# Layer 3 of the last pair but one in layer 0's banks and buffers, and an order of its own for the last periods

## The reference

```
x = L0(x, adj)   8 heads, masked softmax(q k^T), four hops z = 0.9 P z + 0.1 v, then layer norm of x + z
x = L1(x, adj)   1 head: softmax(x Wq Wk^T x^T / 16) x Wv Wo + bo, then layer norm of x + that
x = L2(x, adj)   8 heads, softmax(q k^T / sqrt(32)) v, times Wo, then layer norm
x = L3(adj, x)   labels 1..4 of adj: weight_d = (adj == d) / count, agg = concat_d(weight_d^T x)
                 out = relu(agg Wd + bd)
                 r = sigmoid(out Wri + x Wrh), z = sigmoid(out Wzi + x Wzh)
                 n = tanh(out Wni + r * (x Wnh)), y = (1 - z) n + z x, then layer norm
```

## Time and profile before

| | us |
|---|---|
| median of three runs (1607.26 to 1608.85) | 1607.68 |
| span of the profiled execution, first to last instruction | 1605.4 |
| PE busy | 1547.1 (96%) |
| DVE busy | 1282.8 (80%) |
| ACT busy | 1237.9 (77%) |
| POOL busy | 697.0 (43%) |

### The profile page before, as it was taken

How to read it: one execution, slowest core, us unless ns; L and a number is a source line. 1 busy time by engine, 2 the same in 40 slices (tenths; PEclk the granted TensorE clock), 3 DMA queues, 4 the chain that set the end, 5 groups by cost and what they waited for, 6 DMA issues and landing times.

```text
span 1605.4 us, 44598 instructions
## 1 busy us (share of the span) xinstructions
PE 1547.1 (96%) x17360; PEld 1405.8 (88%) x17360; DVE 1282.8 (80%) x3164; ACT 1237.9 (77%) x4074; POOL 697.0 (43%) x710
## 2 busy tenths in 40 slices
PE   7888999999999999999999999999999999999986
PEld 6777999899899989998998999899899999998875
DVE  3676888888888888888888888888888888888764
ACT  4677887787888788888878788887878888787652
POOL 1344444434454444445444444544444444444411
PEclk7999999999999999999999999999999999999999
DMA  5100000111110011011001101100110110000000
GB/s 201 34 25 28 28 28 15 34 35 29 34 35 28 15 35 34 28 35 35 27 15 35 35 28 35 34 28 15 35 35 28 35 35 27 15 28 25 18 8 13
DMA packets 71425, 51.64 MB, mean 32 GB/s; under 512 B 4400, under 2 KB 69936, under 8 KB 70576
## 3 DMA queue, kind: packets, MB, share of 16 engines
q1 hardware_dynamic: 71216, 48.79, 10.0%
HBM read 40.39 MB, written 8.39 MB: 30 GB/s over the span
## 4 chain that ended last, share of the span: by engine, by line
PE 67%; ACT 28%; DVE 2%; issue 1%; DMA 1%; POOL 0%; SPq 0%; POOLq 0%; DVEq 0%; ACTq 0%
ACT E L706 9%; PE bank_A L400 7%; ACT E L770 7%; PE bank_B L400 7%; PE bank_B L629 6%; PE bank_A L444 6%; PE bank_C L400 5%; PE bank_B L444 4%; PE bank_A L629 3%; PE bank_A L418 3%; PE bank_B L412 3%; ACT PT L712 2%; PE bank_A L430 2%; PE bank_X L550 2%; PE bank_A L528 2%; PE bank_B L438 2%
## 5 line engine op out<-in xcount | busy, mean ns | idle before, releaser
L850 POOL TENSOR_TENSOR E<-E,rsum 128x512 f32<-128x512 f32 x256 | 270.7, 1058 | 472.5 <-DVE rsum L1041 317.6
L858 POOL TENSOR_TENSOR rstd<-var,minus_half 128x2 f32<-128x2 f32 x128 | 93.7, 741 | 407.9 <-DVE var L995 407.9
L712 ACT ACTIVATE PT<-bank_C 128x512 f32<-128x512 f32 x128 | 85.8, 670 | 59.9 <-PE bank_C L438 59.9
L1002 DVE TENSOR_SCALAR y<-y,mv,rstd 128x256 f32<-128x256 f32 x192 | 93.0, 527 | 25.8 <-POOL rstd L858 25.8
L943 DVE COPY_PREDICATED_SCALAR bank_A<-absent,fill 128x512 f32 x128 | 92.3, 742 | 15.2 <-PE bank_B L430 14.4
L400 PE MATMUL bank_A<-xT_hi,w_hi 128*128 128x256 f32 x384 | 99.7, 284 | 0.0
L400 PE MATMUL bank_A<-xT_hi,w_lo 128*128 128x256 f32 x384 | 97.1, 277 | 0.0
L943 DVE COPY_PREDICATED_SCALAR bank_B<-absent,fill 128x512 f32 x128 | 94.7, 740 | 0.0
L770 ACT ACTIVATE E<-bank_A,nmax 128x128 f32<-128x128 f32 x256 | 92.4, 402 | 2.5 <-DVE nmax L1037 2.5
L706 ACT ACTIVATE E<-bank_B,nmax 128x128 f32<-128x128 f32 x256 | 94.2, 435 | 0.0
L706 ACT ACTIVATE E<-bank_A,nmax 128x128 f32<-128x128 f32 x256 | 90.8, 382 | 4.1 <-DVE nmax L946 4.1
(11 more groups left out here) (225 smaller groups left out, 6299.3 us busy)
## 6 DMA issues: line engine op xcount, KB each, us to landing
xt_in<-in_xt SPq DMA_DIRECT2D x64, 128.0 KB, 2.3
absent<-in_adj SPq DMA_DIRECT2D x64, 128.0 KB, 2.7
x_in<-in_x SPq DMA_DIRECT2D x32, 256.0 KB, 3.0
out<-y SPq DMA_DIRECT2D x32, 256.0 KB, 2.2
adj<-in_adj SPq DMA_DIRECT2D x32, 128.0 KB, 3.3
adjT<-in_adjt SPq DMA_DIRECT2D x32, 128.0 KB, 3.1
stage<-in_weights SPq DMA_DIRECT2D x3, 1024.0 KB, 11.3
row<-in_rows SPq DMA_DIRECT2D x1, 1024.0 KB, 7.9
```

The lines of the kernel that those rows point to most:

```text
L712: nc.scalar.activation(PT0[:, part].rearrange("p g c n -> p (g c n)"), C0[:, :], ACT.Copy, scale=1.0 - ALPHA).then_inc(pt0_ready.sem, 1)
L850: nc.gpsimd.tensor_tensor(e, e, rs[:, part].unsqueeze(2).to_broadcast([P, SB, P]), ALU.mult).then_inc(e_sig.sem, 1)
L858: nc.gpsimd.tensor_tensor(rstd[part][:], var[part][:], minus_half[:], ALU.pow)\
L1002: a = nc.vector.tensor_scalar(y[part][:, g, :], src[g], mv[part][:, g, 0:1], rstd[part][:, g:g + 1], ALU.subtract, ALU.mult)
```

## The change

Three things change. First, layer 3's buffers and banks become a named tuple `Layer3`, of which there are two: `main`, the old ones, and `spare`, which lies in layer 0's banks A0 and B0 and in layer 0's buffers (`PT0`, `E0`, `qT0`, `kT0`, `zT0`, `nmax0`, `esum0`, `x_in`). `layer3(it)` gives `spare` for pair 30 (`SPARE = ROUNDS - 2`) and `main` for all others. Where `n3` and `cnt` waited for the pair before, `wait_free3` lets pair 30 wait for `y_sum[0]` of pair 31 (the end of layer 0 of the last pair), and pair 31 for pair 29. Second, the periods from 32 on no longer come from `ORDER`: each engine has a list `TAIL`, in which `lab@1` means step `lab` of the pair one before the last. Third, the eight entries of `IDLE` in the second half of the run go, with their 92 transposes.

```diff
 IDLE = {("p0", 0, 0): 10, ("n1", 0, 0): 12, ("g1", 0, 0): 10, ("p0", 2, 1): 17, ("p1", 0, 0): 9,
-        ("g1", 0, 1): 17, ("p0", 2, 2): 17, ("p0", 3, 2): 8, ("g1", 0, 2): 17, ("p0", 2, 3): 17, ("p0", 3, 3): 8,
-        ("n2", 0, ROUNDS - 1): 8, ("mixt", 0, ROUNDS - 3): 10, ("out", 0, ROUNDS - 2): 7,
-        ("mixt", 0, ROUNDS - 2): 12, ("n3", 0, ROUNDS - 1): 18, ("lab", 0, ROUNDS - 1): 17,
-        ("out", 0, ROUNDS - 1): 7, ("mixt", 0, ROUNDS - 1): 13}
+        ("g1", 0, 1): 17, ("p0", 2, 2): 17, ("p0", 3, 2): 8, ("g1", 0, 2): 17, ("p0", 2, 3): 17, ("p0", 3, 3): 8,}
+TAIL_FROM = 32
+TAIL = {
+    "tensor": [
...
+        "lab.2@2 cnt@1 lab.3@2 agg.2@2 s02.1@-2 agg.3@2 lab@1 out@2 lab.1@1 agg@1 nh@2 p2 lab.2@1 rh@2 agg.1@1 ri@2",
+        "agg.2@1 p2.1 lab.3@1 ni@2 p2.2 p2.3 z@2 agg.3@1 hop2 hop2.1 out@1 cnt wo2 mixt@2 wo2.1 rh@1 nh@1 ri@1 ni@1",
+        "n3 z@1 lab lab.1 agg agg.1 lab.2 lab.3 agg.2 mixt@1 agg.3 out nh rh ri ni z mixt",
...
+SPARE = ROUNDS - 2
+Layer3 = namedtuple("Layer3", "A B BA xT xT_hi xT_lo xw_hi xw_lo agg oT oT_hi oT_lo rT zT nT degree rcnt y")
 def periods(engine):
 
     steps = table(engine)
-    for n in range(ROUNDS + LAST_LAG):
+    for n in range(TAIL_FROM):
         for step, part, lag in steps:
             if 0 <= n - lag < ROUNDS + EXTRA.get(step, 0):
                 yield step, part, n - lag
+    for token in " ".join(TAIL[engine]).split():
+        name, _, back = token.partition("@")
+        step, _, part = name.partition(".")
+        yield step, int(part or 0), ROUNDS - 1 - int(back or 0)
...
+        main = Layer3(A3, B3, (B3, A3), xT3, xT_hi[3], xT_lo[3], xw_hi, xw_lo, agg, oT, oT_hi, oT_lo, rT, zT, nT,
+                      degree, rcnt, y[3])
+        spare = Layer3(A0, B0, (B0, A0), sx, sx_hi, sx_lo, s_hi, s_lo, s_agg, so, so_hi, so_lo, qT0, kT0, zT0,
+                       s_degree, s_rcnt, x_in)
+        def layer3(it):
+            return spare if it == SPARE else main
...
+        def wait_free3(eng, signal, it, k):
+            if it == SPARE:
+                wait(eng, y_sum[0], ROUNDS - 1, G)
+            elif it > SPARE:
+                wait(eng, signal, it - 2, k)
+            else:
+                wait_before(eng, signal, it, k)
...
                     wait(pe, nrm_ready[2], it, 1)
-                    wait_before(pe, nrm_ready[3], it, 1)
-                    transpose_y(A3, y[2]).then_inc(n_t[3].sem, 1)
+                    wait_free3(pe, nrm_ready[3], it, 1)
+                    transpose_y(layer3(it).A, y[2]).then_inc(n_t[3].sem, 1)
```

More of the change, by code:

```diff
@@ L1 @@
+from collections import namedtuple
 from contextlib import ExitStack
@@ L92 @@
 }
+TAIL_FROM = 32
+TAIL = {
+    "tensor": [
[6 rows of a table added]
+    ],
+    "scalar": [
[8 rows of a table added]
+    ],
+    "gpsimd": [
[4 rows of a table added]
+    ],
+    "vector": [
[14 rows of a table added]
+    ],
+    "sync": [
+        "ld_adj.2@2 ld_x@1 ld_adj.1@1 ld_adj.3@3 ld_adj ld_adj.1 ld_adj.3@2 ld_adj.2@1 store@5 ld_x ld_adj.2 store@4",
+        "ld_adj.3@1 ld_adj.3 store@3 store@2 store@1 store",
+    ],
+}
 def table(engine):
@@ L627, in _ @@
                     for kc in range(NC):
-                        for j, (a, w) in enumerate(((xT_hi, w_hi), (xT_lo, w_hi), (xT_hi, w_lo))):
-                            mm = nc.tensor.matmul(BA3[part % 2][:, :], a[3][:, kc, g * P:(g + 1) * P],
+                        for j, (a, w) in enumerate(((at.xT_hi, w_hi), (at.xT_lo, w_hi), (at.xT_hi, w_lo))):
+                            mm = nc.tensor.matmul(at.BA[part % 2][:, :], a[:, kc, g * P:(g + 1) * P],
                                                   w[:, n:n + 2, kc, :], start=kc == 0 and j == 0,
@@ L637, in _ @@
                     for d in range(2):
-                        for xs in (xw_hi, xw_lo):
-                            mm = nc.tensor.matmul(BA3[part % 2][:, d * D:(d + 1) * D], wT[it % 2][:, g, 2 * pair + d],
-                                                  xs[:, part % 2, d], start=xs is xw_hi, stop=xs is xw_lo)
+                        for xs in (at.xw_hi, at.xw_lo):
+                            mm = nc.tensor.matmul(at.BA[part % 2][:, d * D:(d + 1) * D], wT[it % 2][:, g, 2 * pair + d],
+                                                  xs[:, part % 2, d], start=xs is at.xw_hi, stop=xs is at.xw_lo)
                     mm.then_inc(agg_t.sem, 1)
@@ L721, in _ @@
                     L = int(step[-1])
-                    bank = (None, X1, A2, A3)[L]
+                    bank = (None, X1, A2, layer3(it).A)[L]
                     wait(act, n_t[L], it, 1)
                     if step[:2] == "hi":
-                        to, ready = xT_hi[L], xhi_ready[L]
+                        to, ready = x_hi_of(L, it), xhi_ready[L]
                     else:
@@ L728, in _ @@
                             wait_before(act, o2, it, G)
-                        to, ready = xT[L], xt32[L]
+                        to, ready = x_of(L, it), xt32[L]
                     for c in range(NC):
@@ L794, in _ @@
                     wait(act, agg_t, it, 2 * part + 1)
-                    nc.scalar.activation(agg[:, part], BA3[0][:, 0:D], ACT.Copy,
-                                         scale=rcnt[:, part, 0:1]).then_inc(first_sum.sem, 1)
+                    nc.scalar.activation(layer3(it).agg[:, part], layer3(it).BA[0][:, 0:D], ACT.Copy,
+                                         scale=layer3(it).rcnt[:, part, 0:1]).then_inc(first_sum.sem, 1)
                 if step == "lab":
@@ L802, in _ @@
                         wait(act, agg_t, it, part - 1)
-                    nc.scalar.activation(xw_hi[:, part % 2].rearrange("p d f -> p (d f)"), BA3[part % 2][:, :],
+                    nc.scalar.activation(layer3(it).xw_hi[:, part % 2].rearrange("p d f -> p (d f)"),
+                                         layer3(it).BA[part % 2][:, :],
                                          ACT.Copy).then_inc(xw_hi_ready.sem, 1)
@@ L861, in _ @@
                     i = (0, 1, None, 2)[part]
-                    to = (xn[0], xn[1], None, y[3])[part]
+                    to = (xn[0], xn[1], None, layer3(it).y)[part]
                     if step == "sc":
@@ L978, in _ @@
                 if step in ("bn", "nrm"):
-                    src = [A3[:, g * D:(g + 1) * D] if part == 3 else y[part][:, g, :] for g in range(G)]
+                    src = [layer3(it).A[:, g * D:(g + 1) * D] if part == 3 else y[part][:, g, :] for g in range(G)]
                 if step == "bn":
@@ L998, in _ @@
                     wait(dve, rstd_ready[part], it, 1)
-                    if part == 3:
+                    if part == 3 and it != SPARE:
                         wait_before(dve, stored, it, 16)
+                    to = layer3(it).y if part == 3 else y[part]
                     for g in range(G):
-                        a = nc.vector.tensor_scalar(y[part][:, g, :], src[g], mv[part][:, g, 0:1],
+                        a = nc.vector.tensor_scalar(to[:, g, :], src[g], mv[part][:, g, 0:1],
                                                     rstd[part][:, g:g + 1], ALU.subtract, ALU.mult)
@@ L1063, in _ @@
                     wait(dve, counted, it, 1)
-                    count = B3[:, 0:2 * G * LABELS].rearrange("p (g d two) -> p g d two", g=G, d=LABELS)
-                    nc.vector.tensor_scalar(degree[:], count[:, :, :, 0], DEG_EPS, None, ALU.add)\
+                    count = layer3(it).B[:, 0:2 * G * LABELS].rearrange("p (g d two) -> p g d two", g=G, d=LABELS)
+                    nc.vector.tensor_scalar(layer3(it).degree[:], count[:, :, :, 0], DEG_EPS, None, ALU.add)\
                         .then_inc(guarded.sem, 1)
```

83 lines of the change are left out of this document (51 added, 32 removed), and 29 rows, old and new, of the table TAIL.

## The result

The changed kernel takes 1596.24 us (median of four runs, 1592.98 to 1598.14), the kernel before 1608.26 (1607.26 to 1611.74): a ratio of 0.9919 with a 95% interval of 0.9901 to 0.9936, 12.0 us faster by the medians and 0.8% by the ratio. The forecast was 1592.0 in a range of 1585.5 to 1600.5. The profiled execution has a span of 1596.3 us and a time of 1598.14, 1.8 above it.

The account below looks back on a forecast made before the run. PE bounds the body, latency of layer 3 passes run one behind the other the end. `n3` of pair 31 at 1554.5, plus 34.8 and 0.4, ends the span at 1589.7; time 1592.0 us, range 1585.5 to 1600.5.

Parts of the forecast that it names:

- The last pass: Layer 3 of pair 31, from its `n3` to the end of the span: 34.8 us as before, plus 0.4.
- The start of the last pass: `n3` of pair 31, forecast at 1554.5 us: 1504.9 plus 44.1 of PE work, 4.3 of waits and 1.2 for handovers.
- the stretch that I took as unchanged: 1466.5 to 1504.9 us, up to `n3` of pair 29: same steps reordered, priced at 0, between −2.2 and +2 us.
- the recorded sum: PE work from `n3` of pair 29 to `n3` of pair 31: 17.2 + 14.0 + 11.0 + 1.9 = 44.1 us.
- The sum of the waits: PE's waits between `n3` of pair 29 and `n3` of pair 31, forecast at 4.3 us in all.
- the walk: Going through the four engines' lists with earlier durations to find PE's waits; it gave 4.3 us.
- The 1.2 us for handovers: Added before `n3` of pair 31 for handovers between engines taken as free at nine or ten places.
- The other branch: Layer 2's norm for pair 31, also needed before its `n3`: ready near 1553.1 us, level with PE at 1553.3.
- The clock: PE's granted clock without fillers: no cost but 0.3 us at the last `mixt`; upper end 7 us.
- half hidden: Rival, chance 0.12: layer 3's two passes block each other in DVE and ACT queues; `n3` of pair 31 at 1563.0, time 1600.5.
- the rivals: Besides half hidden: PE never waiting, 1584 (0.04); one clock fall, 1599 (0.05); clock staying low (0.04); no effect, 1607 (0.01).

## Why the prediction was right, and where its sum was off

**The mechanism.** It held: `n3` of pair 31, plus one pass, is the time, and the second pass of layer 3 beside the first moved that `n3` by 13.1 us. The banks alone gave a ratio of 0.9986, the fillers' removal alone a loss, and the order can't run without the banks.

**The last pass.** Forecast 35.2 us, measured 35.33. The last `mixt` at half the clock was named with 0.3 us and then left out of the sum; it cost 0.35. `bn.3` of pair 30 ahead of `acc.4` was put at 0.35: `out` waits 1.30 us for the last `acc`. The stretch from `n3` to the last `mixt` is 26.03 us against 25.91, so nearly all of that was hidden. `z` of pair 30 in the gap cost nothing, as forecast, and the experiment that takes it out of the gap lost 2.65.

**The start of the last pass.** From the mark the forecast was 1554.5 − 1413.7 = 140.8 us, measured 143.75: 3.0 us too soon. Half of it is the stretch that I took as unchanged. `n3` of pair 29 comes 92.52 us after the mark instead of 91.15, because it waits for the norm of pair 28 in bank A3, which the recorded sum does not have; `mixt` of pair 28 itself stands behind a wait of 1.11. DVE and PE in order of time:

```profile
1505.11 0.69 DVE L1209 SCALAR_TENSOR_TENSOR oT<-oT,nT 128x512 f32<-128x512 f32 x1
...
1506.55 0.76 DVE L1079 BATCH_NORM_STATS2 stats<-bank_A 128x6 f32<-128x256 f32 x2 [0.66 <-PE bank_A L756]
...
1508.60 1.00 DVE L1096 TENSOR_SCALAR y<-bank_A,mv,rstd 128x256 f32<-128x256 f32 x2 [0.81 <-POOL rstd L950]
```

`mixt` at 1505.85, statistics, POOL's power, `nrm.3` from 1508.60, and then `n3` at 1509.74 with 0.59 us of wait: a chain of 3.9 us that the new order has on PE's path. The experiment with the old period 32 shows these 1.3 us, and that 0.9 of them were paid back behind.

The other half is the PE work between the two `n3`: 44.1 us in the sum, 47.3 in the stretch of 51.3. The sum of the waits was right, 4.0 us idle against a forecast of 4.3, but their places only in part. Around `agg.2` and `s02.1` of pair 29 PE waits 0.61 and 0.46 us, where 1.8 was forecast; at `lab` of pair 29 0.26 instead of 1.1, at `out` and `ni` of pair 29 nothing instead of 0.7, at `hop2` of pair 31 0.88 instead of 0.4; and the longest, 0.99 us before `k2` of pair 31, was not in the walk at all. That these errors cancel is luck. The missing 3.2 us of work, read as the distance from one step's start to the next, less waits: eight `agg` take 4.9 us instead of 3.8, eight `lab` 12.0 instead of 11.2, the rest of layer 2 of pair 30 2.5 instead of 1.9, eight projections of layer 3 11.3 instead of 11.0, and `wo2`, `z`, `s02` and `cnt` 0.2 each at most. The blocks were priced at their bare length: `agg` at 0.47 where the earlier trace rows shows 0.74, of which I took the rest for the drain. From its start to the next start and less waits, an `agg` takes 0.47 us in two of the eight cases, 0.57 in one and 0.63 to 0.72 in five; what makes the difference was not tested. The 1.2 us for handovers covered 1.2 of it.

**The other branch.** The norm of layer 2 was forecast ready at 1553.1 with PE there at 1553.3, level. In the profile after, DVE:

```profile
1556.22 0.75 DVE L1079 BATCH_NORM_STATS2 stats<-y 128x6 f32<-128x256 f32 x2
...
1558.73 0.74 DVE L1096 TENSOR_SCALAR y<-y,mv,rstd 128x256 f32<-128x256 f32 x2 [0.69 <-POOL rstd L950]
1559.54 0.99 DVE L1096 TENSOR_SCALAR y<-bank_A,mv,rstd 128x256 f32<-128x256 f32 x2
```

The statistics, at 1544.42 before, now run at 1556.22, and the norm ends at 1559.47, 1.5 us before PE takes up `n3` at 1560.97. But this was the wrong end of the branch. The last line is `nrm.3` of pair 29, which reads bank A3, ends at 1560.53 and must be over before `n3` of pair 31 may write there. The prediction did not count it: in its own terms the bank would have been free about 1 us after the 1553.1, past the 1553.3 at which it had PE arrive, and the 1.2 us added for handovers hid that. In the run PE is 0.4 us later than the bank, so its queue still sets the start, by a hair. `ni` moved away gained 0.05 of 1.4 for this reason. The second bank set uncouples neighbouring pairs, and pairs 29 and 31 still share one.

**The clock.** No fall before the last `mixt` in the profiled executions, as forecast; the longest wait of PE before it is 1.30 us. The trace of before was right against the Trainium skill's rule ("TensorE: Matmul & The Clock Gate", Part 4: PE-mode transpose) that transposes do not count as busy: without the 92 transposes the clock fell and the end took 3.3 us more in the trace. "The 92 fillers cost 0 where PE waits anyway" was true, but said only half: where they stood they were also worth at least 3.3 us.

**The rest.** 3.1 us less gained at the end turn the forecast of 15.7 into 12.6, against 12.0 by the medians. The remainder of the distance between 1592.0 and 1596.24, 1.1 us, is within the spread between executions, which the mark shows to be up to 5 us. By the time alone the result lies as far from the forecast (4.24 us) as from *half hidden* at 1600.5 (4.26). The trace decides between them: the extra waits of 9.7 us that this rival needs are absent, and `n3` of pair 31 comes 143.75 us after the mark, where the forecast had 140.8 and half hidden 149.3. None of the rivals came. The time stands 1.8 us above the span of the profiled execution, where the forecast had put 2.3.

What stays open: whether a DVE order exists that has both the old place of `n3` of pair 29 and an early `xT_lo`, and whether `n3` of pair 31 gains if pair 29's `nrm.3` runs ahead of layer 2's norm or `n3` gets another bank. Neither was tried.

## What to carry to other kernels

At the end of a pipeline a stage that holds one item at a time makes the last items run one behind the other, though every engine has room; the buffers and banks of a stage that has already ended give it a second place at no cost in memory, but only an order that uses it brings the gain. Look also for the items that still share a place: here the last pair and the one two before it. A walk through the engines' lists gave the sum of the waits, though not their places, and bare block lengths are too short where blocks alternate: price a block by the distance from its start to the next start in a stretch that mixes steps as the new one will. To judge a change in the last tenth of a run, measure from a mark that both programs share, and profile more than one execution where the clock can fall.

## What the runs showed of the hardware

- Transposes of the identity hold the granted clock: the kernel before with 92 of them keeps 1.00 where, without them, it is 0.50 (1.2 GHz) for 13 us. With 13 of them ahead of it the last `mixt` takes 0.65 us; without them it took 1.01, 1.11 and 1.12 us in three traces and 0.66 in a fourth, behind the same 2.38 us without work.
- The clock can fall though no wait is long, and the waits alone do not tell whether it will. With the spare banks in the old order it went to 0.50 at 1528 us, after waits of 0.30, 0.90 and 0.76 us from 1523.4 on; the kernel before has the same waits at the same steps and kept 1.00, as did the changed kernel with waits of 1.11, 0.59 and 0.99 us.
- It may fall during idle time or just behind it: at the start of the kernel before it is at 0.50 from 10.4 us on the earlier trace rows, and PE, idle since 8.1, starts again only at 11.05, and with `z` ahead 2.75 us of idle are still at 1.00 and the next matmuls run at 0.50. It stayed there for about 3 us in that kernel, and for 13 in another, where three waits of 2.19, 3.23 and 2.75 us came in a row.
- The start, with weights and graphs coming in at 145 and 166 GB/s and the clock at 0.57 and 0.76 between 30 and 38 us in two traces, holds the difference between executions: with one program the first `mixt` stands at 191.2 and 196.4 us, and the mark at 1412.05 and 1417.22.
